# Cross attention scores with the keys on partitions, instead of queries on partitions and transposed probabilities

## The chip, the cores and the metric

The kernel runs on one core of a Trainium2 chip. The time is device microseconds of one execution of the whole program. Timed three times, the kernel before took 3029.02, 3022.6 and 3023.99 us, median 3023.99 us.

## The reference, cut to what matters

A decoder block with three residual parts, each followed by a layer norm: causal self attention (32 heads of 16), cross attention, and a feed forward with a gated low-rank part. The batch is 4 sequences of 256 queries and width 512. The change touches the cross attention alone: 32 heads of 128, 8 key and value heads, 1601 context rows.

```python
scale = 1.0 / sqrt(HDIM)                                   # HDIM = 128
q = (query @ Wq + bq).reshape(B, L, NKV, G, HDIM)          # L = 256, NKV = 8, G = 4
k_, v_ = split(kv @ Wkv + bkv, 2)                          # kv: 1601 rows
scores = einsum('blkgd,bmkd->bkglm', q, k) * scale
attn = softmax(scores)
o = einsum('bkglm,bmkd->blkgd', attn, v)
return o.reshape(B, L, NHEAD * HDIM) @ Wo + bo
```

## The kernel before, in words

One batch element after the other (`for b in range(nb)`), each in three stages: self attention, cross attention, feed forward. Five engines work from programs of their own (`block.tensor` for PE, `block.scalar` for ACT, `block.vector` for DVE, `block.gpsimd` for POOL, `block.sync` for SP, which issues the DMAs) and meet only at semaphores. An engine takes its instructions in order: a wait holds everything behind it.

In the cross attention almost every product is made of three matmuls in fp32r, high times high, high times low, low times high (`mm`, L960). So each operand is split: ACT writes the high part and DVE the low part. The matmuls are grouped in jobs, each into one PSUM bank of a ring of three (`RING`, `freed`): K jobs (keys, four per key head, 12 matmuls of 400 columns), V jobs (values, 13 per pair of key heads, 12 of 256 columns), Q jobs (one per head, 12 of 256), O jobs (output, two per two heads, 6 of 512). `run_job` (L1079) is PE's part, `job_high` (L630) ACT's, `job_low` (L806) DVE's.

A head passes through seven slots `s`, each for two tiles of 128 keys (the last slot has one tile, of 65). The order of jobs and slots is written out by `slot_jobs`.

- `scores` (L1063): queries on partitions, 128 queries at a time, 24 matmuls of 400 or 402 columns per head into four banks (`sp4`).
- `reduce_pair` (L832, the reduce is L837): DVE takes the negative maximum over 800 keys, four times per head; `exponent_bias` (L844) joins them.
- `exponentials` (L652, the activation is L657): ACT writes exp(scale*s - scale*max) to `pbuf`, four passes of 800 columns per head, which also give the row sums.
- `turn_weights` (L1124, L1132): PE transposes the probabilities, 26 tiles of 128x128 per head, so that the keys lie on partitions. ACT makes `ph` (L684), DVE makes `pl` (L884), 512 columns per slot.
- `weigh` (L1136): 39 matmuls of 256 columns per head sum into the one bank `dn`. ACT copies it out (`take_heads_sum`, L666), DVE multiplies by the reciprocals of the sums (`normalize`, L860), which PE spreads over the partitions by two transposes (`spread_reciprocals`, L1159). POOL then adds the bias and splits the result (`finish_head`, L509 to L522).

While the first batch element is worked on, POOL and SP also split the weights of the cross attention into high and low parts, three pieces per head for the first 23 heads (`split_weight`, L499 to L507).

## Time and profile before

| | us |
|---|---|
| median of three runs | 3023.99 |
| the profiled execution | 3015.1 |
| its span, first to last instruction | 3013.3 |
| PE busy | 2897.0 |
| DVE busy | 1778.3 |
| ACT busy | 1448.1 |
| POOL busy | 519.2 |

"PE" counts matmuls, "PEld" the loads of the stationary operand that run beside them. A matmul's duration is a latency: its successor starts long before it ends. The time that a matmul costs is the distance between two starts, which the prediction calls its pitch; for DVE and ACT too a successor can start a little before the predecessor's end. The granted clock is that of TensorE, 1.00 is 2.4 GHz and 0.50 is 1.2 GHz.

### The profile page before, as it was taken

Reading aid. Unit: us, or ns where it says so; the run is one execution under the profiler, and the core shown is the slowest. Engines: PE = TensorE matmul, PEld = TensorE weight load, DVE = VectorE, ACT = ScalarE, POOL = GpSimd, SP = SyncE. Lnnn points to the kernel's source line nnn. Section 1 sums busy time; section 2 is a strip of 40 time slices with the busy share of each in tenths; the row PEclk is TensorE's granted clock in tenths of the full one; section 3 lists DMA queues with packets and bytes.
Section 4 is the critical chain, followed back from the end, with each engine's and each line's share of the span. In section 5 each row is a group of like instructions: output and inputs, shape, how many; then the busy total and the mean of one; then the engine's idle time right before and its main releaser. Section 6 shows DMA issues by size and latency. Waiting matters only on the chain.

```text
span 3013.3 us, 54054 instructions
## 1 busy us (share of the span) xinstructions
PE 2897.0 (96%) x20400; PEld 2727.9 (91%) x20400; DVE 1778.3 (59%) x3596; ACT 1448.1 (48%) x3368; POOL 519.2 (17%) x639
## 2 busy tenths in 40 slices
PE   7899999998899999999889999999988999999997
PEld 6799999998689999999778999999977899999995
DVE  5466666655656565665564656565656565656564
ACT  5454444444545444544364545444536454545453
POOL 4233443301101011111120101010112010101011
PEclk9999999999999999999999999999999999999998
DMA  5455555413212121211321212121232121212113
GB/s 196 141 183 199 182 202 177 164 50 143 89 37 71 57 78 64 78 64 63 127 88 34 71 57 85 57 78 64 78 116 90 36 78 50 79 56 85 57 50 108
DMA packets 97870, 284.69 MB, mean 94 GB/s; under 512 B 9936, under 2 KB 18256, under 8 KB 94416
## 3 DMA queue, kind: packets, MB, share of 16 engines
q1 hardware_dynamic: 97616, 281.24, 27.2%
q8 instruction: 168, 2.75, 0.4%
q14 instruction: 86, 0.70, 0.1%
HBM read 237.16 MB, written 44.04 MB: 93 GB/s over the span
## 4 chain that ended last, share of the span: by engine, by line
PE 91%; DVE 2%; issue 2%; ACT 2%; DMA 1%; POOL 1%; SPq 0%; ACTq 0%; DVEq 0%; POOLq 0%
PE bank L960 36%; PE sp L960 21%; PE dn L960 21%; PE bank L1132 12%; PE bank L1159 1%; PE sp L1031 1%; ACT pn L608 1%; DVE nmx L780 1%; DMA wqk<-in_ws 0%; PE sp L966 0%; ACT pt L614 0%; DVE pn L789 0%; DVE xres L728 0%; DVE stats L719 0%; DMA raw<-in_ctx_t 0%
## 5 line engine op out<-in xcount | busy, mean ns | idle before, releaser
L684 ACT ACTIVATE ph<-bank 128x512 fp32r<-128x512 f32 (+1 forms) x896 | 504.6, 567 | 693.2 <-PE bank L1132 689.7
L884 DVE TENSOR_TENSOR pl<-bank,ph 128x512 fp32r<-128x512 f32 (+1 forms) x896 | 580.2, 648 | 158.0 <-ACT ph L684 146.8
L837 DVE TENSOR_REDUCE mneg<-sp 128x1 f32<-128x800 f32 (+1 forms) x512 | 507.4, 992 | 81.1 <-PE sp L960 61.6
L960 PE MATMUL dn<-ph,vh 128*128 128x256 f32 (+1 forms) x1664 | 541.8, 326 | 0.0
L1132 PE MATMUL bank<-cst,pbuf 128*128 128x128 f32 (+1 forms) x3328 | 509.4, 272 | 1.4
L657 ACT ACTIVATE pbuf<-sp,mb 128x800 f32<-128x800 f32 (+1 forms) x512 | 470.8, 929 | 27.5 <-DVE mb L844 27.4
L960 PE MATMUL dn<-ph,vl 128*128 128x256 f32 (+1 forms) x1664 | 465.4, 280 | 0.0
L960 PE MATMUL dn<-pl,vh 128*128 128x256 f32 (+1 forms) x1664 | 464.8, 279 | 0.0
L1132 PEld LDWEIGHTS bank<-cst,pbuf 128*128 128x128 f32 (+1 forms) x3328 | 404.2, 140 | 41.1 <-DVE pl L884 6.1
L518 POOL TENSOR_SCALAR orw<-orw,cst 128x256 f32<-128x256 f32 x128 | 118.6, 927 | 1768.6 <-DVE orw L860 1768.6
L960 PE MATMUL sp<-kh,qh 128*128 128x400 f32 (+1 forms) x1024 | 363.5, 355 | 5.2 <-issue 4.8
L960 PE MATMUL sp<-kl,qh 128*128 128x400 f32 (+1 forms) x1024 | 354.2, 346 | 0.0
L960 PE MATMUL sp<-kh,ql 128*128 128x400 f32 (+1 forms) x1024 | 352.1, 344 | 0.0
L960 PEld LDWEIGHTS dn<-pl,vh 128*128 128x128 f32 (+1 forms) x1664 | 316.3, 190 | 0.0
L960 PEld LDWEIGHTS dn<-ph,vh 128*128 128x128 f32 (+1 forms) x1664 | 314.6, 189 | 0.3
L960 PEld LDWEIGHTS dn<-ph,vl 128*128 128x128 f32 (+1 forms) x1664 | 312.5, 188 | 0.0
L960 PE MATMUL bank<-wvx,ctxh 128*128 128x256 f32 (+1 forms) x1664 | 298.4, 280 | 0.0
L960 PE MATMUL bank<-ctxh,wk 128*128 128x400 f32 (+1 forms) x1024 | 290.5, 346 | 3.1 <-DVE xres L804 3.1
L960 PEld LDWEIGHTS bank<-wvx,ctxh 128*128 128x128 f32 (+1 forms) x1664 | 254.6, 184 | 0.0
L960 PE MATMUL bank<-wvx,ctxl 128*128 128x256 f32 (+1 forms) x832 | 234.2, 282 | 0.0
L639 ACT ACTIVATE kh<-bank,cst 128x400 fp32r<-128x400 f32 (+1 forms) x128 | 76.4, 597 | 307.1 <-PE bank L960 307.1
L820 DVE SCALAR_TENSOR_TENSOR kl<-bank,cst,kh 128x400 fp32r<-128x400 f32 (+1 forms) x128 | 81.1, 634 | 239.2 <-ACT kh L639 239.2
(126 smaller groups left out, 4841.9 us busy)
## 6 DMA issues: line engine op xcount, KB each, us to landing
wqx<-wq SPq DMA_DIRECT2D x128, 512.0 KB, 3.3
wox<-wo SPq DMA_DIRECT2D x64, 1024.0 KB, 4.9
wk<-wk SPq DMA_DIRECT2D x32, 512.0 KB, 3.3
wvx<-wv SPq DMA_DIRECT2D x16, 1024.0 KB, 5.7
raw<-in_ctx_t SPq DMA_DIRECT2D x48, 200.0 KB, 2.5
wqk<-in_ws SPq DMA_DIRECT2D x17, 513.0 KB, 3.9
raw<-in_wq_in SPq DMA_DIRECT2D x32, 256.0 KB, 3.7
wq<-hib SPq DMA_DIRECT2D x32, 256.0 KB, 2.0
```

What stands on the lines that cost most here:

```text
L518: nc.gpsimd.tensor_scalar(o, o, bias, None, ALU.add).then_inc(oh_ok, 1)
L608: nc.scalar.activation(pn[:, n % 3, a:z], s_bank[n % 5][:, a:z], ACT.Exp, bias=nmx[:, n % 3, qb:qb + 1], accum_out=sm[:, n % 3, qb:qb + 1] ...
L639: nc.scalar.activation(kh[:, a:a + n], src[:, 0:n], ACT.Identity, bias=cst[:, 2 * p + C_BK + kv:2 * p + C_BK + kv + 1]).then_inc(*done)
L657: nc.scalar.activation(pbuf[:, n % 2, tb, key:key + w], spf[:, col:col + w], ACT.Exp, bias=mb[:, n % 2, tb:tb + 1], scale=XSCALE, accum_ou ...
L684: nc.scalar.activation(ph[0:rows, k % PH, 0:cols], ring_bank(b, "turn", h, s)[0:rows, 0:cols], ACT.Copy).then_inc(hi_ok, 1)
L780: nc.vector.tensor_reduce(nmx[:, n % 3, qb:qb + 1], s_bank[n % 5][:, a:z], AX.X, ALU.max, negate=True).then_inc(s_mx, 1)
L820: nc.vector.scalar_tensor_tensor(kl[:, a:a + n], src[:, 0:n], cst[:, 2 * p + C_BK + kv:2 * p + C_BK + kv + 1], kh[:, a:a + n], ALU.add, AL ...
L837: nc.vector.tensor_reduce(mneg[:, n % 2, tb, pair:pair + 1], spf[:, col:col + w], AX.X, ALU.max, negate=True).then_inc(mx_ok, 1)
L884: nc.vector.tensor_tensor(pl[0:rows, k % PH, 0:cols], ring_bank(b, "turn", h, s)[0:rows, 0:cols], ph[0:rows, k % PH, 0:cols], ALU.subtract ...
L960: return nc.tensor.matmul(dst, lhs, rhs, start=first, stop=final)
L1031: last = nc.tensor.transpose(s_turn[:, z:z + P], pn[:, (n - 2) % 3, a:a + P], ident)
L1132: last = nc.tensor.transpose(bank[r % RING][0:w, col:col + P], pbuf[:, n % 2, tb, i * P:i * P + w], ident)
```

## The change

Scores are now computed with the keys on partitions: `kh` and `kl` tiles of 128 keys are stationary, the 256 queries of the head move, 39 matmuls per head. Each slot's scores go into one of two banks. ACT copies them to SBUF (`kept_s`); DVE keeps a running maximum over the key blocks (`mxa`). At the head's end PE transposes `mxa` (four transposes), DVE reduces it (`mcol`), PE spreads the maxima over all partitions (two transposes) and ACT copies them to `mrow`. POOL subtracts `mrow` from the kept scores, slot by slot. ACT then takes the exponential twice: into `ph` (rounded to fp32r) and in full into one of two PSUM banks (`pbank`). DVE makes `pl` from the two and adds the block to a running sum `sua`. Four fp32 matmuls with one moving column of ones give the row sums. `turn_weights` and the 26 transposes of probabilities per head are gone. The ring of banks for jobs goes from three to two, `ph` and `pl` from three to four buffers.

The order of all engines is now a list of slots `g`, 239 per batch element; every step of head h and slot s stands at `g = 7*h + s + offset`: scores at -13, subtraction at -4, exponentials at -3, low part and sum at -2, `weigh` at 0. The steps done once per head have fixed places too (`MAX_TURN` and the others). DVE takes a job's low part one slot after PE runs the job. The weight pieces of the first batch element are placed at slots 0, 2 and 4 of each head, for POOL and for SP, and Q jobs run one head earlier than before.

The diff, cut to its core (lines left out at "..."):

```diff
-RING = 3
-PH = 3
+RING = 2
+PH = 4
...
-    + [("Q", 0, 1)] + [("V", 0, i) for i in range(5, KT)]
+KEYS = [[(i, LAST if i == KT - 1 else P) for i in (2 * s, 2 * s + 1) if i < KT] for s in range(NSL)]
+SCORE, SHIFT, EXP, LOW, VALUE = -13, -4, -3, -2, 0
+MAX_TURN, MAX_COL, MAX_ROW, SUM_COL, SUM_ROW, HEAD_SUM, HEAD_END = -6, -5, -4, 5, 6, 7, 8
+SLOTS = range(SCORE, NSL * (NHB - 1) + HEAD_END + 1)
+def slot_of(g, start):
+    h, s = divmod(g - start, NSL)
+    return [(h, s)] if 0 <= h < NHB else []
+def head_of(g, start):
...
+O_SLOTS = [(3, 3, 5), (2, 5, 6), (2, 5, 6), (3, 1, 3)]
+def jobs_by_slot():
+    jobs = {g: [] for g in SLOTS}
+    for i in range(KT):
+        jobs[SCORE + i].append(("V", 0, i))
+    for p in range(1, NP):
+        for i in range(KT):
+            jobs[NSL * (NHD * p - 1) + 1 + i * 10 // 12].append(("V", p, i))
+    for c in range(1, XKV):
+        for j, (head, s) in enumerate(((-3, 4), (-3, 5), (-3, 6), (-2, 1))):
+            jobs[NSL * (G * c + head) + s].append(("K", c // 2, c % 2 * len(KCH) + j))
+    for h in range(1, NHB):
+        jobs[NSL * h + SCORE - 6].append(("Q",) + divmod(h, NHD))
+    for k in range(NHB // 2 - 1):
+        after, *slots = O_SLOTS[k % 4]
+        for tb, s in enumerate(slots):
+            jobs[NSL * (2 * k + after) + s].append(("O", k // 4, 2 * (k % 4) + tb))
     return jobs
-def ring_uses():
...
-        pbuf = sb("pbuf", [P, 2, TB, LKP])
+        kept_s = sb("kept_s", [P, 2, KT, S])
...
+        bank = [ctx.enter_context(nc.psum_tensor(f"bank{i}", [P, 512], F32)) for i in range(3)]
...
+        sbank, pbank, mbank = [bank[2][:, :], sp4[:, 0, :]], [sp4[:, 1, :], sp4[:, 2, :]], sp4[:, 3, :]
...
+            def shift_scores(b, h, s):
+                n = b * NHB + h
+                i, z = 2 * s, 2 * s + len(KEYS[s])
+                pool.wait_ge(mr_ok, n + 1)
+                pool.wait_ge(cp_ok, n * NSL + s + 1)
+                nc.gpsimd.tensor_tensor(kept_s[:, n % 2, i:z, :], kept_s[:, n % 2, i:z, :],
+                                        mrow[:, n % 2, :].unsqueeze(1).broadcast_to([P, z - i, S]), ALU.subtract).then_inc(sb_ok, 1)
...
+                for g in SLOTS:
+                    for h, s in slot_of(g, SHIFT):
+                        shift_scores(b, h, s)
+                    for h in head_of(g, HEAD_END):
+                        finish_head(b, h)
+                    h, s = divmod(g, NSL)
+                    if b == 0 and 0 <= h < NHB and s in PIECE_SLOTS:
+                        k = NM * SA_W + HEAD_W * h + PIECE_SLOTS.index(s)
+                        if k < W_N:
                             split_weight(k)
...
+                def keep_scores(h, s):
                     n = b * NHB + h
-                    act.wait_ge(mb_ok, at(n, TB, tb + 1))
-                    for pair, (col, key, w) in enumerate(PAIR_AT):
-                        nc.scalar.activation(pbuf[:, n % 2, tb, key:key + w], spf[:, col:col + w], ACT.Exp,
-                                             bias=mb[:, n % 2, tb:tb + 1], scale=XSCALE,
-                                             accum_out=sums[:, n % 2, tb, pair:pair + 1]).then_inc(exp_ok, 1)
+                    k = n * NSL + s
+                    src, dst = sbank[k % 2], kept_s[:, n % 2, 2 * s:2 * s + len(KEYS[s]), :].rearrange("p t q -> p (t q)")
+                    act.wait_ge(sc_mm, k + 1)
+                    if s == NSL - 1:
+                        nc.scalar.activation(dst, src[:, 0:S], ACT.Identity, bias=cst[:, C_TAIL:C_TAIL + 1]).then_inc(cp_ok, 1)
+                    else:
+                        nc.scalar.activation(dst, src[:, :], ACT.Copy).then_inc(cp_ok, 1)
+                def keep_max(h):
+                    n = b * NHB + h
+                    act.wait_ge(mr_mm, n + 1)
+                    if n >= 2:
+                        act.wait_ge(sb_ok, (n - 1) * NSL)
+                    nc.scalar.activation(mrow[:, n % 2, :], mbank[:, 0:S], ACT.Copy).then_inc(mr_ok, 1)
+                def exponentials(h, s):
+                    n = b * NHB + h
+                    k, cols = n * NSL + s, S * len(KEYS[s])
+                    src = kept_s[:, n % 2, 2 * s:2 * s + len(KEYS[s]), :].rearrange("p t q -> p (t q)")
+                    act.wait_ge(sb_ok, k + 1)
+                    if k >= PH:
+                        act.wait_ge(pv_mm, k - PH + 1)
+                    nc.scalar.activation(ph[:, k % PH, 0:cols], src, ACT.Exp, scale=XSCALE).then_inc(ph_ok, 1)
+                    if k >= 2:
+                        act.wait_ge(su_ok, k - 1)
+                    nc.scalar.activation(pbank[k % 2][:, 0:cols], src, ACT.Exp, scale=XSCALE).then_inc(pr_ok, 1)
...
+                for g in SLOTS:
+                    for h in head_of(g, HEAD_SUM):
+                        take_heads_sum(h)
+                    for h, s in slot_of(g, SCORE):
+                        keep_scores(h, s)
+                    for h in head_of(g, MAX_ROW):
+                        keep_max(h)
+                    for h, s in slot_of(g, EXP):
+                        exponentials(h, s)
+                    for j in JOBS[g]:
+                        if j[0] != "O":
+                            job_high(*j)
                 deviation(b, 1)
...
+                def maximum(h, s):
                     n = b * NHB + h
-                    dve.wait_ge(sc_mm, at(n, 4, 2 * tb + pair + 1))
-                    col, _, w = PAIR_AT[pair]
-                    nc.vector.tensor_reduce(mneg[:, n % 2, tb, pair:pair + 1], spf[:, col:col + w], AX.X, ALU.max,
-                                            negate=True).then_inc(mx_ok, 1)
-                def exponent_bias(h, tb):
+                    k, cols = n * NSL + s, S * len(KEYS[s])
+                    dve.wait_ge(cp_ok, k + 1)
+                    if s == 1:
+                        dve.wait_ge(tm_mm, n)
+                        last = kept_s[:, n % 2, 0:2, :].rearrange("p t q -> p (t q)")
+                    else:
+                        dve.wait_ge(mx_ok, n * (NSL - 1) + s - 1)
+                        last = mxa[:, 0:cols]
+                    if s == NSL - 1:
+                        nc.vector.tensor_tensor(mxa[0:LAST, 0:cols], sbank[k % 2][0:LAST, 0:cols], mxa[0:LAST, 0:cols],
+                                                ALU.max).then_inc(mx_ok, 1)
+                    else:
+                        nc.vector.tensor_tensor(mxa[:, 0:cols], sbank[k % 2][:, 0:cols], last, ALU.max).then_inc(mx_ok, 1)
+                def row_maxima(h):
                     n = b * NHB + h
-                    dve.wait_ge(mx_ok, at(n, 4, 2 * tb + 2))
-                    nc.vector.tensor_scalar(mb[:, n % 2, tb:tb + 1], mneg[:, n % 2, tb, 0:1], mneg[:, n % 2, tb, 1:2], XSCALE,
-                                            ALU.min, ALU.mult).then_inc(mb_ok, 1)
+                    dve.wait_ge(tm_mm, n + 1)
+                    dve.wait_ge(mr_mm, n)
+                    nc.vector.tensor_reduce(mcol[:, :], mbank.rearrange("p (a n) -> p a n", a=TB), AX.X, ALU.max).then_inc(mc_ok, 1)
+                def low_and_sum(h, s):
+                    n = b * NHB + h
+                    k, cols = n * NSL + s, S * len(KEYS[s])
+                    src = pbank[k % 2][:, 0:cols]
+                    dve.wait_ge(pr_ok, k + 1)
+                    dve.wait_ge(ph_ok, k + 1)
+                    if k >= PH:
+                        dve.wait_ge(pv_mm, k - PH + 1)
+                    nc.vector.tensor_tensor(pl[:, k % PH, 0:cols], src, ph[:, k % PH, 0:cols], ALU.subtract).then_inc(pl_ok, 1)
+                    if s == 0:
+                        dve.wait_ge(sx_mm, n)
+                        nc.vector.tensor_copy(sua[:, 0:cols], src).then_inc(su_ok, 1)
+                    else:
+                        dve.wait_ge(su_ok, k)
+                        nc.vector.tensor_tensor(sua[:, 0:cols], src, sua[:, 0:cols], ALU.add).then_inc(su_ok, 1)
                 def row_reciprocals(h):
                     n = b * NHB + h
-                    dve.wait_ge(exp_ok, at(n, 4, 4))
-                    nc.vector.tensor_reduce(ssum[:, n % 2, :], sums[:, n % 2, :, :], AX.X, ALU.add).then_inc(rs_ok, 1)
-                    dve.wait_ge(rs_ok, at(n, 2, 1))
-                    nc.vector.reciprocal(rs[:, n % 2, :], ssum[:, n % 2, :]).then_inc(rs_ok, 1)
+                    dve.wait_ge(sx_mm, n + 1)
+                    dve.wait_ge(rd_mm, n)
+                    nc.vector.reciprocal(rs[:, :], mbank[:, 0:TB]).then_inc(rs_ok, 1)
                 def normalize(h):
                     n = b * NHB + h
...
+                for g in SLOTS:
+                    for j in JOBS.get(g - 1, ()):
+                        job_low(*j)
+                    for h, s in slot_of(g, LOW):
+                        low_and_sum(h, s)
+                    for h in head_of(g, MAX_COL):
+                        row_maxima(h)
+                    for h in head_of(g, SUM_COL):
+                        row_reciprocals(h)
+                    for h in head_of(g, HEAD_SUM):
+                        normalize(h)
+                    for h, s in slot_of(g, SCORE):
+                        if s:
+                            maximum(h, s)
                 for j in LAST_JOBS:
                     job_low(*j)
...
+                def scores(h, s):
                     n = b * NHB + h
                     p = h // NHD
-                    pe.wait_ge(exp_ok, at(n, 4, 2 * tb + pair - 1))
-                    pe.wait_ge(freed, ring(b, "job", "Q", p, h % NHD) + RING + 1)
+                    k = n * NSL + s
+                    if k >= 2:
+                        a, z = divmod(k - 2, NSL)
+                        pe.wait_ge(cp_ok, k - 1)
+                        pe.wait_ge(mx_ok, a * (NSL - 1) + z)
+                    pe.wait_ge(freed, ring(b, "Q", p, h % NHD) + RING + 1)
                     if h % G == 0:
-                        pe.wait_ge(freed, ring(b, "job", "K", p, h % NHD // G * len(KCH) + 2 * pair + 1) + RING + 1)
-                    q = slice(tb * P, (tb + 1) * P)
-                    for col, key, w in SP_AT[2 * pair:2 * pair + 2]:
-                        dst = spf[:, col:col + w]
-                        mm(dst, qh[:, h % G, q], kh[:, key:key + w], True, False)
-                        mm(dst, ql[:, h % G, q], kh[:, key:key + w], False, False)
-                        last = mm(dst, qh[:, h % G, q], kl[:, key:key + w], False, True)
+                        pe.wait_ge(freed, ring(b, "K", p, h % NHD // G * len(KCH) + chunk_of(s)) + RING + 1)
+                    for e, (i, w) in enumerate(KEYS[s]):
+                        dst, keys = sbank[k % 2][0:w, e * S:(e + 1) * S], slice(i * P, i * P + w)
+                        mm(dst, kh[:, keys], qh[:, h % G, :], True, False)
+                        mm(dst, kh[:, keys], ql[:, h % G, :], False, False)
+                        last = mm(dst, kl[:, keys], qh[:, h % G, :], False, True)
                     last.then_inc(sc_mm, 1)
+                def turn_maxima(h):
+                    n = b * NHB + h
+                    pe.wait_ge(mx_ok, (n + 1) * (NSL - 1))
+                    if n >= 2:
+                        pe.wait_ge(nm_ok, n - 1)
+                    for tb in range(TB):
+                        for e in range(2):
+                            col = (2 * tb + e) * P
+                            last = nc.tensor.transpose(mbank[:, col:col + P], mxa[:, e * S + tb * P:e * S + (tb + 1) * P], ident)
+                    last.then_inc(tm_mm, 1)
+                def spread_maxima(h):
+                    n = b * NHB + h
+                    pe.wait_ge(mc_ok, n + 1)
+                    for tb in range(TB):
+                        last = nc.tensor.transpose(mbank[:, tb * P:(tb + 1) * P], mcol[:, tb:tb + 1].broadcast_to([P, P]), ident)
+                    last.then_inc(mr_mm, 1)
+                def sum_rows(h):
+                    n = b * NHB + h
+                    pe.wait_ge(su_ok, (n + 1) * NSL)
+                    pe.wait_ge(mr_ok, n + (2 if h + 1 < NHB else 1))
+                    for tb in range(TB):
+                        for e in range(2):
+                            last = mm(mbank[:, tb:tb + 1], sua[:, e * S + tb * P:e * S + (tb + 1) * P], cst[:, C_ONE:C_ONE + 1],
+                                      e == 0, e == 1)
+                    last.then_inc(sx_mm, 1)
...
-                def turn_weights(h, s):
-                    n, r = b * NHB + h, ring(b, "turn", h, s)
...
+                for g in SLOTS:
+                    for h, s in slot_of(g, SCORE):
+                        scores(h, s)
+                    for h in head_of(g, MAX_ROW):
+                        spread_maxima(h)
+                    for h in head_of(g, SUM_ROW):
+                        spread_reciprocals(h)
+                    for j in JOBS[g]:
+                        run_job(*j)
+                    for h, s in slot_of(g, VALUE):
+                        weigh(h, s)
+                    for h in head_of(g, MAX_TURN):
+                        turn_maxima(h)
+                    for h in head_of(g, SUM_COL):
+                        sum_rows(h)
                 for j in LAST_JOBS:
```

## Rows read from the trace of the kernel before

**Rows 1.** Chain that ended last: share of the span by engine.
```profile
PE 91%; DVE 2%; issue 2%; ACT 2%; DMA 1%; POOL 1%; SPq 0%; ACTq 0%; DVEq 0%; POOLq 0%
```
**Rows 2.** Windows: one element's head stage, then eight heads of elements 0 and 1.
```profile
core 0: us, PE busy (x) PEld busy (x) DVE busy (x) ACT busy (x) POOL busy (x), PEclk, DMA share, GB/s
866.60:1476.30 609.70, 609.25 (x4424) 593.24 (x4424) 370.46 (x652) 294.31 (x624) 64.03 (x93) 1.00 0.19 66
...
446.32:601.66 155.34, 155.28 (x1126) 151.33 (x1126) 93.86 (x166) 74.00 (x158) 56.49 (x67) 1.00 0.50 175
1035.57:1190.91 155.34, 155.28 (x1127) 151.34 (x1126) 93.85 (x166) 73.99 (x158) 16.52 (x24) 1.00 0.20 69
```
**Rows 3.** Timeline of PE, 256 and 400 columns: start us, duration us, instruction.
```profile
404.49 0.35 PE L960 MATMUL sp<-kh,qh 128*128 128x400 f32 x1
...
406.69 0.35 PE L960 MATMUL bank<-ctxh,wk 128*128 128x400 f32 x1
...
868.88 0.40 PE L960 MATMUL bank<-wvx,ctxh 128*128 128x256 f32 x2
...
875.97 0.34 PE L960 MATMUL sp<-kh,qh 128*128 128x400 f32 x1
```
**Rows 4.** Timeline of PE: four transposes, `weigh` after them, four fp32 matmuls.
```profile
400.77 0.60 PE L1132 MATMUL bank<-cst,pbuf 128*128 128x128 f32 x4
401.12 0.37 PE L960 MATMUL dn<-ph,vh 128*128 128x256 f32 x1
401.33 0.28 PE L960 MATMUL dn<-pl,vh 128*128 128x256 f32 x1
...
19.83 0.61 PE L960 MATMUL bank<-wv,xt 128*128 128x128 f32 x4
```
**Rows 5.** Timeline of DVE, instructions back to back.
```profile
470.38 0.69 DVE L884 TENSOR_TENSOR pl<-bank,ph 128x512 fp32r<-128x512 f32 x1
470.99 0.41 DVE L860 TENSOR_TENSOR orw<-bank,orw 128x256 f32<-128x256 f32 x1
471.41 0.99 DVE L837 TENSOR_REDUCE mneg<-sp 128x1 f32<-128x801 f32 x1
```
**Rows 6.** Timeline of ACT, instructions back to back.
```profile
445.65 0.60 ACT L684 ACTIVATE ph<-bank 128x512 fp32r<-128x512 f32 x1
446.14 0.93 ACT L657 ACTIVATE pbuf<-sp,mb 128x800 f32<-128x800 f32 x1
446.95 0.20 ACT L657 ACTIVATION_READ_ACCUMULATOR pbuf<-sp,mb 128x1 f32 x1
```
**Rows 7.** Groups by shape, POOL: busy us, mean ns, idle before.
```profile
L507 POOL TENSOR_TENSOR lob<-raw,hib 128x512 fp32r<-128x512 f32 x80 | 103.5, 1294 | 6.4
...
L522 POOL TENSOR_TENSOR ol<-orw,oh 128x256 fp32r<-128x256 f32 x128 | 94.7, 740 | 11.0
```
**Rows 8.** Timeline, last head of element 1: last `weigh` matmul, its copy, the multiplication.
```profile
1475.96 0.28 PE L960 MATMUL dn<-ph,vl 65*128 65x256 f32 x1
...
1476.28 0.38 ACT L666 ACTIVATE orw<-dn 128x256 f32<-128x256 f32 x1 [1.38 <-PE dn L960]
...
1476.69 0.42 DVE L860 TENSOR_TENSOR orw<-bank,orw 128x256 f32<-128x256 f32 x1 [1.34 <-ACT orw L666]
```
**Rows 9.** Timeline: PE resumes after waiting for DVE's `ql`.
```profile
121.46 0.48 DVE L825 SCALAR_TENSOR_TENSOR ql<-bank,cst,qh 128x256 fp32r<-128x256 f32 x1 [0.73 <-ACT qh L645]
122.04 0.42 PE L960 MATMUL sp<-kh,qh 128*128 128x400 f32 x1 [1.20 <-issue]
122.30 0.34 PE L960 MATMUL sp<-kh,ql 128*128 128x400 f32 x1
```
**Rows 10.** Windows: self attention, and after the wait at a stage's end.
```profile
20.00:100.00 80.00, 64.91 (x492) 53.36 (x491) 56.45 (x184) 52.90 (x193) 38.52 (x40) 1.00 0.58 180
...
1476.30:1480.00 3.70, 0.60 (x4) 0.43 (x3) 0.42 (x1) 1.64 (x2) 2.04 (x3) 1.00 1.04 428
1480.00:1484.00 4.00, 4.00 (x12) 2.91 (x10) 0.69 (x1) 0.00 (x0) 0.00 (x0) 0.57 0.87 358
```

More of the change, by code:

```diff
@@ L120 @@
+JOBS = jobs_by_slot()
+JOB_AT = {j: i for i, j in enumerate(FIRST_JOBS + [j for g in SLOTS for j in JOBS[g]] + LAST_JOBS)}
 NJ = len(JOB_AT)
@@ L161, in raw_of_weight @@
     return NM * len(SA_RAW) + k - NM * SA_W
-def head_pieces(h):
-    first = NM * SA_W + HEAD_W * h
-    return range(min(first, W_N), min(first + HEAD_W, W_N))
 NSH = NM * HB
@@ L1272, in lay_out @@
     consts[:, C_EPS] = EPS
+    consts[LAST:, C_TAIL] = NEG
+    consts[:, C_ONE] = 1.0
     consts[:, C_BK:C_BK + XKV] = i["L0_xattn_bkv"][:XKV * XD].reshape(XKV, XD).T
```

291 lines of the change are left out of this document (91 added, 200 removed).

## The prediction, made before the changed kernel was run

> **What bounds the kernel now.** I read the chain of waits first: 91% of the span is PE [rows 1]. Then the windows. The cross attention's head stage of one batch element, from the first scores to the last spread of reciprocals, lasts 609.7 us, and PE is busy for 609.25 of them at full clock; eight heads take 155.34 us, 19.4 each, the same in element 0 and element 1 [rows 2]. DVE is busy for 60% of that, ACT for 48%, POOL for 11% (36% in element 0). So what the stage costs is the sum of PE's pitches, and every other engine is hidden. Four such stages are 2439 of 3013 us, and the change is inside them alone.
>
> Pitches of PE: 12 score matmuls of 400 columns lie between 404.49 and 406.69, 0.183 us each; 60 of 256 columns between 868.88 and 875.97, 0.118 each [rows 3]. Four transposes take 0.35 us to the next start, and the matmul behind them costs 0.21 instead of 0.12, so a group is 0.44 and a pair 0.22 [rows 4].
>
> **What PE saves.** Per head, out: six groups of four transposes and one pair, 6 x 0.44 + 0.22 = 2.86 us. Scores: 24 x 0.183 = 4.39 become 39 x 0.118 = 4.60, plus 0.21. In: four transposes of `mxa` 0.44, two of `mcol` 0.22, and `sum_rows`. For its fp32 matmuls with one column no row exists. Four fp32 matmuls of 128 columns take 0.61 us, a latency of 0.28 included, so 0.11 each, 0.53 with the changeover [rows 4]; the lower end is the transposes' 0.35 for four. I take 0.50. Net: -2.86 + 0.21 + 0.44 + 0.22 + 0.50 = -1.49 us per head, 48 us per element, 191 us in all. PE's work in a stage falls from 610 to 562 us. This is the whole possible gain.
>
> **What the others get.** DVE is busy 93.9 / 8 = 11.7 us per head [rows 2]. Out go four reduces of 0.99 and small ones of 0.57 together. In come six maxima and seven sums. Two 512-column passes in a row cost 0.61 each, not the 0.69 of their duration [rows 5], and the passes of 256 columns 0.34: 3.4 + 4.0 us. The reduce of 512 columns is 0.99 less 288 columns at (0.69 - 0.41) / 256, about 0.7. That gives 15.3 us per head, 80% of what a head takes. ACT: 74 / 8 = 9.3, less four exponentials of 0.9 and seven high parts of 3.3 together, plus seven copies (3.3), `mrow` (0.3) and fourteen exponentials. One of 512 columns lies between 0.52 (0.81 for 800, scaled) and 0.60 (a whole copy) [rows 6]; I take 0.57: 13.6 us. POOL: 16.5 / 8 = 2.1 for `finish_head` [rows 2], plus 6 x 1.29 + 0.74 = 8.5 for the subtraction [rows 7]: 10.6. In element 0 the weight pieces add (56.5 - 16.5) / 8 = 5.0: 15.6.
>
> No engine passes PE on the average of 562 / 32 = 17.6 us. But PE's work is uneven: a head with no jobs but Q has about 12 us of it, the head with eight V jobs 23, and the other engines keep nearly the same load in all. In a light slot PE has 1.4 us (two times six matmuls), DVE 1.8 (three passes). Two score banks bind them: PE may start slot g only when DVE has finished slot g-2.
>
> **The new waits of PE.** I stepped the schedule through, slot by slot: each instruction starts when its engine is free and its semaphores are in, with the pitches above and 0.06 us per semaphore. It adds these, per element:
> - Reciprocals. `spread_reciprocals` stands in the slot after `sum_rows`, behind six score matmuls (0.70). From the sum on, DVE first does the copy that starts the next head's `sua`, because that copy waits for `sum_rows` too, and then the reciprocal: 0.23 for the matmul's latency beyond its pitch and a semaphore, 0.61, the reciprocal 0.15, and the way back to PE 0.15: 1.15 us. PE waits 0.45, 32 times: 14 us.
> - The bank `dn`. `weigh` of the next head starts one slot after the last `weigh`; between stand only three score matmuls. The copy starts 0.32 us after the last matmul does and lasts 0.38 [rows 8], and ACT can be inside an exponential. The wait is 0.3 to 2 us, 0.65 on the mean, 28 times: 18 us. Before, two slots of other work stood in between.
> - DVE late with a maximum or a low part: in three of eight heads, and above all in the 13 slots behind the last scores, where PE has 12 us of work and DVE two passes per slot. Together 12 us.
> - Each wait costs a restart: PE's first pitch after one is 0.26 instead of 0.18, and it starts 0.10 after DVE's end [rows 9]. 85 x 0.09 = 8 us.
>
> Sum: 562 + 52 = 614 against 610, so +4 us per element, +16 in all. In element 0, POOL's 15.6 us stand beside heads of 15.3 to 16.6 us, and its lateness reaches ACT: +4. DMAs: SP waits for the same jobs as before, but a Q load is issued a head earlier, and the pieces stand two slots apart instead of one behind the other; the self attention and feed forward stages are not touched. I cost these at nothing, hidden by two heads of distance. What ends up on the profiled execution's 3015.1 us is +20, 3035 us; the median of the runs stands 9 us higher, so 3042 is the number I give for a median.
>
> **Two rules weighed.** DVE's rows show a successor starting 0.61 us after a pass that lasts 0.69 [rows 5]. The Trainium skill, VectorE: DVE Perf Modes, section "The DRAIN you can't avoid", says that the next operation starts only when the pipe has emptied. By that rule every pass would cost its duration, rival B below; the rows before speak against it. The other is the clock. In self attention PE is busy 81% of the time, the rest in many waits, and the granted clock stays at 1.00; after 3.1 us of idleness at a stage's end it is 0.57, partly at the 1.2 GHz level [rows 10]. The Trainium skill, TensorE: Matmul & The Clock Gate, section "A second HAM failure mode: psum-queue depth-cycling", says that frequent short idles between groups of matmuls make the clock swing. By it this change would lose clock, rival C; the row at 81% speaks against it, since I expect 91%.
>
> **Rivals.**
> - Forecast: gain on PE's pitches, given back in waits; -5 to +55 us. 48%.
> - A, faster: the waits are hidden better than I step them, with semaphores of 0.03 us and no restart cost: 604 us per element, -20 in all. If DVE cost nothing at all, the stepping gives -72; the saved work of 191 us is never reached, because ACT's and POOL's links remain. Time: 2990 to 3018. For it: 191 us of PE work really go, and idle time on DVE and ACT remains. 28%.
> - B, slower through DVE: with several semaphores per pass and its own chains (`sua`, `mxa`), a pass costs 0.69. Then DVE has 16.5 us per head and the light heads go by DVE; the stepping gives 630 us per element, +82, so 3124. It decides from a pitch of 0.63 on: each 0.02 us adds 15. For it: three semaphores stand before each low part, where the rows have passes behind one. Against it: the rows. 20%.
> - C, the clock: a few per cent of the matmuls at half speed, +50 to +150. 4%.
> - The change would not do what it says only in that fp32 matmuls with one column cost far more than 0.11, say 0.25 each: +0.5 us per head, +60. It is within the range, for B's numbers.
>
> **How the numbers follow.** Faster by over 0.2% (6 us, about what a measurement of this kernel can tell) takes A and a piece of the forecast's lower end: 0.30. Within: 0.15. Slower: 0.55. The range leaves out A's far end and half of B and C: 2990 to 3115 us.
>
> **What would show it.** PE busy in a head stage falls to about 91% of it, its work to 562 us. Waits of PE `dn` for ACT's `orw` copy, about 0.65 us, once per head, and of the spread for DVE's `rs`, 0.45 us. DVE's passes 0.61 us apart when back to back; DVE busy near 15 us per head and POOL's subtraction at 1.29 us. Heads with V jobs near 24 us, heads without jobs near 15 to 16. I am wrong if PE's waits per stage are under 40 us or over 70, if `sum_rows` takes over 0.8 us, or if the granted clock inside the stage leaves 1.00.

## The result and the profile after

The changed kernel took 3050.99 us (median of 4 runs, 3042.88 to 3052.90), the kernel before beside it 3023.30 us (4 runs, 3015.25 to 3029.02). The ratio is 1.0087, with a 95% interval of 1.0070 to 1.0104: slower, by less than 1%. The prediction said 3042, slower, and 3051 lies within its range. The profiled execution took 3042.88 us, its span 3041.1, so the spans differ by 27.8 us where the steps gave 20.

The page of the kernel after, parts 1 and 4 (busy time, and the chain that ended last); the chain answers to [rows 1].

```profile
PE 2831.5 (93%) x20784; PEld 2619.2 (86%) x20784; DVE 2171.2 (71%) x4492; ACT 1906.0 (63%) x4264; POOL 1570.0 (52%) x1535
...
PE 78%; issue 7%; ACT 6%; POOL 3%; DVE 3%; DMA 2%; DVEq 0%; SPq 0%; ACTq 0%; POOLq 0%
```

PE's part in the chain falls from 91% to 78%, and what took its place is issue, ACT, POOL and DVE: not one new bound, but many small links. The windows of the kernel after say where the time is: the head stages of elements 0 to 3, first scores to last spread of reciprocals (in the kernel after, three `weigh` matmuls stand behind that spread, and the window ends with them). They answer to the first of [rows 2]. (Columns: window, its length, then the busy time and the number of instructions of PE, PEld, DVE, ACT and POOL, the granted clock, the DMA share, GB/s.)

```profile
124.10:744.90 620.80, 592.59 (x4520) 566.80 (x4520) 469.26 (x876) 409.24 (x847) 453.14 (x453) 1.00 0.47 158
881.10:1495.70 614.60, 591.98 (x4520) 565.31 (x4520) 468.76 (x876) 408.52 (x847) 327.38 (x317) 1.00 0.21 71
1631.90:2246.60 614.70, 592.10 (x4520) 565.30 (x4520) 468.74 (x876) 408.57 (x847) 327.49 (x317) 1.00 0.20 71
2382.90:2997.60 614.70, 592.11 (x4520) 565.38 (x4520) 468.87 (x876) 408.55 (x847) 327.42 (x317) 1.00 0.19 67
```

Four stages of 609.7 became 620.8 and three of about 614.7: 11.1 + 4.9 + 5.0 + 5.0 = 26 of the 27.8 us. Per head DVE is busy 468.8 / 32 = 14.6 us, ACT 12.8, POOL 10.2 (14.2 in element 0), where the prediction has 15.3, 13.6, 10.6 and 15.6. The granted clock rounds to 1.00 in all four; the places inside them where it is lower come below, under rival C. PE counts as busy for 592 us, which is more than the sum of its pitches: a matmul's recorded duration runs on for 0.16 us behind its pitch, so every wait is partly covered by "busy" in this column. The waits themselves, in element 1's stage (who waited for whom, us in total, times, longest):

```profile
PEld dn L1012 <- ACT orw L713: 20.2, 28, 1.0
PEld sp L1232 <- DVE rs L917: 8.8, 32, 0.9
PEld sp L1143 <- DVE mxa L883: 4.9, 10, 0.8
PEld sp L1151 <- DVE mcol L893: 2.2, 2, 1.8
```

I read them at PEld, the weight load, because it is the first thing that a waiting group of matmuls issues: 36 us in four places, those that were forecast, and 5.5 us in scraps, 41.6 in all. Before, the same rows of a head stage add up to 3.4 us. The timeline of PE shows the first two and the new fp32 matmuls (start us, duration us, then what it idled for).

```profile
1053.31 0.95 PE L1012 MATMUL sp<-cst,sua 128*128 128x1 f32 x8
1054.12 0.36 PE L1012 MATMUL bank<-qh,kh 128*128 128x256 f32 x1
1054.32 0.28 PE L1012 MATMUL bank<-ql,kh 128*128 128x256 f32 x1
...
1054.78 0.28 PE L1012 MATMUL bank<-qh,kl 128*128 128x256 f32 x1
1055.12 0.43 PE L1232 MATMUL sp<-cst,rs 128*128 128x128 f32 x2
...
1486.57 0.28 PE L1012 MATMUL dn<-ph,vl 65*128 65x256 f32 x1
1487.33 0.38 PE L1012 MATMUL dn<-ph,vh 128*128 128x256 f32 x1 [0.47 <-ACT orw L713]
```

`sum_rows` writes four matmuls, and the trace has eight records of them, from 1053.31 to 1054.12: 0.81 us, and the next matmul's pitch is 0.20 instead of 0.115. That is 0.90 us per head where the prediction has 0.50. The spread of the reciprocals starts at 1055.12 where 1054.90 was its turn. Across the boundary of two heads, 1486.57 to 1487.33, PE loses 0.64 us to the copy out of bank `dn`.

### The profile page after: what moved, and what is told of

It reads as the page before. It is cut to its first block, busy times and chain, and to the rows that moved or that the text cites. A ratio compares the mean times of both kernels' runs of the same rounds, so it can differ in the third digit from the quotient of the medians.

```text
span 3041.1 us, 60253 instructions
## 1 busy us (share of the span) xinstructions
PE 2831.5 (93%) x20784; PEld 2619.2 (86%) x20784; DVE 2171.2 (71%) x4492; ACT 1906.0 (63%) x4264; POOL 1570.0 (52%) x1535
## 4 chain that ended last, share of the span: by engine, by line
PE 78%; issue 7%; ACT 6%; POOL 3%; DVE 3%; DMA 2%; DVEq 0%; SPq 0%; ACTq 0%; POOLq 0%
PE bank L1012 41%; PE dn L1012 18%; PE sp L1012 14%; PE sp L1143 2%; ACT ph L702 2%; POOL kept_s L524 1%; ACT orw L713 1%; PE sp L1232 1%; PE sp L1083 1%; PE sp L1151 1%; ACT pn L629 1%; POOL lob L516 1%; DVE nmx L819 1%; POOL orw L536 0%; DMA wqk<-in_ws 0%
## 5 line engine op out<-in xcount | busy, mean ns | idle before, releaser
L524 POOL TENSOR_TENSOR kept_s<-kept_s,mrow 128x512 f32<-128x512 f32 (+1 forms) x896 | 1061.1, 1214 | 539.8 <-ACT mrow L692 539.8
L904 DVE TENSOR_TENSOR pl<-sp,ph 128x512 fp32r<-128x512 f32 (+1 forms) x896 | 577.0, 644 | 43.3 <-ACT sp L705 42.8
L702 ACT ACTIVATE ph<-kept_s 128x512 fp32r<-128x512 f32 (+1 forms) x896 | 534.8, 597 | 35.1 <-POOL kept_s L524 30.3
L705 ACT ACTIVATE sp<-kept_s 128x512 f32<-128x512 f32 (+1 forms) x896 | 506.3, 565 | 3.5 <-DVE sua L910 2.2
L910 DVE TENSOR_TENSOR sua<-sp,sua 128x512 f32<-128x512 f32 (+1 forms) x768 | 487.7, 635 | 0.0
L684 ACT ACTIVATE kept_s<-bank 128x512 f32<-128x512 f32 x384 | 229.0, 596 | 330.6 <-PE bank L1012 330.6
L684 ACT ACTIVATE kept_s<-sp 128x512 f32<-128x512 f32 x384 | 229.6, 598 | 254.8 <-PE sp L1012 254.8
L1012 PE MATMUL bank<-qh,kh 128*128 128x256 f32 (+1 forms) x832 | 245.2, 295 | 10.1 <-DVE ql L864 5.2
L1012 PE MATMUL sp<-qh,kh 128*128 128x256 f32 (+1 forms) x832 | 243.2, 292 | 0.2
L1012 PE MATMUL sp<-qh,kl 128*128 128x256 f32 (+1 forms) x832 | 232.9, 280 | 0.0
```

What stands on the lines that cost most here:

```text
L524: nc.gpsimd.tensor_tensor(kept_s[:, n % 2, i:z, :], kept_s[:, n % 2, i:z, :], mrow[:, n % 2, :].unsqueeze(1).broadcast_to([P, z - i, S]), ...
L684: nc.scalar.activation(dst, src[:, :], ACT.Copy).then_inc(cp_ok, 1)
L702: nc.scalar.activation(ph[:, k % PH, 0:cols], src, ACT.Exp, scale=XSCALE).then_inc(ph_ok, 1)
L705: nc.scalar.activation(pbank[k % 2][:, 0:cols], src, ACT.Exp, scale=XSCALE).then_inc(pr_ok, 1)
L904: nc.vector.tensor_tensor(pl[:, k % PH, 0:cols], src, ph[:, k % PH, 0:cols], ALU.subtract).then_inc(pl_ok, 1)
L910: nc.vector.tensor_tensor(sua[:, 0:cols], src, sua[:, 0:cols], ALU.add).then_inc(su_ok, 1)
```

## The experiments

Two theories stand against each other, and every expectation names both. Theory 1 is the prediction's: PE's pitches plus the short loops through other engines that PE must wait for, `dn` (ACT), `rs`, `mxa` and `mcol` (DVE), with `sum_rows` at 0.90. Theory 2 has the stage set by the rate at which DVE, ACT and POOL get through their work, the waits being only where that shows. All edits are to the kernel after, except in the last. The ratios are to the kernel before, timed beside each version. In the tables of windows a "stage" is that of element 1, as above.

### The Q job between two heads

```
-        jobs[NSL * h + SCORE - 6].append(("Q",) + divmod(h, NHD))
+        jobs[max(SCORE, NSL * h + SCORE - 8)].append(("Q",) + divmod(h, NHD))
```

SCORE - 6 is -19, slot 2 of a head; -21 is slot 0, where the job stands ahead of the head's first `weigh`.

> The changed kernel with one edit: each Q job (12 matmuls, 1.4 us of PE) stands in the slot in which PE now waits for the copy out of the bank dn, two slots earlier than in the change. Theory 1, PE's waits are serial links that other PE work could cover: the wait of the next head's weigh for the copy, 20 us per batch element in the trace of the changed kernel, and its restarts all but vanish, and nothing else replaces them: 15 to 25 us per element, 60 to 90 us in all, 2960 to 2990 us. Theory 2, DVE's passes set the rate and PE's wait is only where it shows: within 10 us of the changed kernel's 3050, with PE's waits moved to the running maximum. In between, since the slot behind is lighter: -30 to -50.

2998.67 us (2993.67 to 3008.06), ratio 0.9924 (0.9898 to 0.9950). The stage:

```profile
868.20:1470.00 601.80, 587.02 (x4516) 564.97 (x4516) 464.67 (x877) 406.94 (x847) 327.71 (x317) 1.00 0.21 72
```

Its waits over the whole span, and under them those of the kernel after:

```profile
PEld sp L1151 <- DVE mcol L893: 43.4, 60, 1.8
...
PEld dn L1012 <- ACT orw L713: 10.2, 17, 1.0
```

```profile
PEld dn L1012 <- ACT orw L713: 86.6, 112, 2.0
PEld sp L1232 <- DVE rs L917: 36.1, 128, 1.0
PEld sp L1143 <- DVE mxa L883: 18.6, 38, 0.8
PEld sp L1151 <- DVE mcol L893: 9.0, 8, 1.8
```

PE does the same work in another order, and 12.8 us per element go, 52 us in all. That is less than the 60 to 90 of theory 1, which expected that nothing would replace the wait for `dn`, and just past the 30 to 50 given for a case in between. The wait for `dn` falls by 76 us, but the wait for `mcol` grows by 34. That is the other side of the same move: slot 2 lies between the turn of the maxima (end of slot 1) and their spread (slot 3), so the job had been the cover of DVE's reduce, and that was its price. A theory of rates alone has no place for either number; the engines' busy times hardly move.

### The reduce of the maxima ahead of the low part on DVE

```
+                    for h in head_of(g, MAX_COL):
+                        row_maxima(h)
                     for h, s in slot_of(g, LOW):
                         low_and_sum(h, s)
-                    for h in head_of(g, MAX_COL):
-                        row_maxima(h)
```

with the Q job moved as above.

> The moved Q jobs again, and on DVE the reduce of the transposed maxima now stands ahead of the low part and sum of its slot instead of behind them. With the Q jobs moved, PE waited 43 us in all for that reduce (31 us of them visible on PE), a wait that came when the slot ahead of the spread lost its Q job. Theory 1, serial links: it goes, 25 to 40 us off the 2999 of the moved Q jobs alone, 2960 to 2975. Theory 2, DVE's rate: the same DVE work in another order gives back less than 10 us, 2990 or more.

2984.37 us (2976.35 to 2985.78), ratio 0.9864 (0.9840 to 0.9887).

```profile
873.40:1469.80 596.40, 587.19 (x4520) 565.75 (x4520) 463.65 (x876) 406.42 (x847) 327.60 (x317) 1.00 0.21 73
```

The wait for `mcol` falls from 43.4 to 2.5 us in the span, and the stage is 5.4 us shorter. The time is above what theory 1 expected and below what theory 2 did. Part of what is missing shows as waits that had come to 1.1 us in the span with the Q job moved alone, for ACT's copy of the scores out of the bank:

```profile
PEld sp L1012 <- ACT kept_s L684: 11.4, 28, 0.5
PEld bank L1012 <- ACT kept_s L684: 10.8, 49, 0.3
```

PE's score matmuls need a bank that ACT has copied. While PE was held elsewhere, the copy was nearly always in time.

### The reciprocal ahead of the copy that starts the next sum

```
                     for h in head_of(g, SUM_COL):
                         row_reciprocals(h)
+                    for h, s in slot_of(g, LOW):
+                        if s == 0:
+                            first_sum(h, s)
```

where `first_sum` is the `tensor_copy` to `sua` that `low_and_sum` did in slot 0; alone first, with the Q job where the change has it.

> The changed kernel with one edit: DVE takes the reciprocal of the row sums before, not after, the copy that starts the next head's running sum. No instruction is added or removed. Theory 1: PE's wait for the reciprocals (9 us per element with 32 restarts of 0.09, so 12) goes, 47 us in all at most, 20 to 45 expected since part of it comes back as a wait for DVE's maximum. Theory 2, DVE's rate: no change, within 8 us, since DVE has the same work.

3032.96 us (10 runs, 3028.12 to 3037.41), ratio 1.0025 (1.0014 to 1.0037), 18 us under the change: short of the 20 to 45 of theory 1, and more than twice the 8 of theory 2.

```profile
884.90:1495.50 610.60, 587.66 (x4520) 564.65 (x4520) 468.67 (x876) 408.62 (x847) 327.45 (x317) 1.00 0.21 72
```

The wait for `rs` falls from 36.1 to 2.8 us; in its place `mxa` rises from 18.6 to 23.6 and waits for `kept_s` appear, the largest with 9.0:

```profile
PEld sp L1149 <- DVE mxa L883: 23.6, 40, 0.8
...
PEld bank L1018 <- ACT kept_s L684: 9.0, 32, 0.3
```

This element gains 4.0 us of the 8.8 that PE waited in it.

### The three moves together

> All three moves: Q jobs two slots earlier, DVE's reduce of the maxima ahead of the low part, DVE's reciprocal ahead of the copy. Theory 1: the gains add, about 12.9 us per element for the first, 6 to 10 for the second, 3.5 to 5 for the third: 588 to 593 us per element and 2945 to 2965 in all, which would be 2% under the kernel before. Theory 2: they overlap, 2975 or more, with waits for the running maximum in their place.

2962.94 us (2958.68 to 2965.07), ratio 0.9794 (0.9775 to 0.9813); the stage:

```profile
865.00:1457.90 592.90, 583.27 (x4516) 565.36 (x4517) 463.79 (x877) 406.16 (x847) 327.71 (x317) 1.00 0.21 73
```

That is inside what theory 1 expected, for the stage and for the time. 21.7 us of the stage are gone, by order alone: the instructions are those of the change. Of 41.6 us of waits in the stage 20.2 are left, above all for `kept_s` (24 + 17 us in the span), `orw` (12) and `mxa` (11).

### Half the row sums

The loop `for e in range(2)` of `sum_rows` runs once, so each row sum covers about half of the keys.

> The changed kernel with the row sums taken over one half of the keys only: two of the four fp32 matmuls with one column per head are left out, so the output's scale is off. In the trace they cost 0.81 us per head for what I had taken as 0.41. If PE's pitches plus its waits make the stage (theory 1), leaving two out takes 0.4 us from each head: 128 x 0.4 = 51 us, 2995 to 3010 us. If DVE sets the rate (theory 2), less than 15 us.

2998.85 us (2997.13 to 3002.32), ratio 0.9916 (0.9894 to 0.9938).

```profile
877.60:1477.80 600.20, 577.13 (x4390) 550.47 (x4391) 468.90 (x877) 408.61 (x847) 328.00 (x317) 1.00 0.21 72
```

52 us under the change, as theory 1 expected. Two matmuls less per head, four records: 14.4 / 32 = 0.45 us, against 0.40 from the timeline, and PE's waits stay what they were (41.8 us in the stage, 41.6 before the edit). So the fp32 matmuls of one column lie wholly on the path, at 0.20 to 0.22 us each.

### POOL's subtraction halved

`i, z = 2 * s, 2 * s + 1` in POOL's subtraction: the first key tile of each pair alone; the second keeps its unshifted scores.

> The changed kernel with POOL's subtraction on the first key tile of each slot only: the second tile keeps its unshifted scores, so the output is not the reference's; POOL has 4.2 us less per head. Theory 1 with POOL as the cause of element 0's longer stage (620.8 us against 614.6 of the others): element 0 falls to about 615, the others stay within 1 us: 5 to 8 us in all. Rival: the splitting of weights, its stores or SP's order delay element 0 in another way: element 0 stays at 620. Second rival: the link POOL to ACT is on the path in every element: all four fall, by 5 us or more each.

3042.77 us (3041.10 to 3045.13), ratio 1.0057 (1.0036 to 1.0078). Elements 0 and 1:

```profile
131.50:746.00 614.50, 591.93 (x4520) 565.24 (x4520) 468.84 (x876) 406.94 (x847) 349.68 (x453) 1.00 0.47 160
882.00:1496.10 614.10, 591.50 (x4519) 564.85 (x4520) 468.80 (x876) 406.94 (x847) 221.91 (x317) 1.00 0.20 71
```

8 us under the change, the upper end of what theory 1 gave. POOL does some 104 us less in each element. Element 0 loses its 6.2 us of excess, element 1 only 0.5. So POOL's rate costs in element 0, where the weight pieces stand beside the subtraction, and hardly anywhere else; not all of the 6.2 us is POOL's, as the part on element 0 below shows. The waits of the kernel after in element 0's stage show the same:

```profile
POOL kept_s L524 <- ACT mrow L692: 89.1, 22, 26.2
...
ACT ph L702 <- POOL kept_s L524: 24.3, 21, 4.6
```

In element 1 POOL waits 150 us for `mrow`, and ACT 2.0 us for POOL: POOL has time there that it lacks in element 0.

### The running sum's adds cut to 8 columns

```
-                        nc.vector.tensor_tensor(sua[:, 0:cols], src, sua[:, 0:cols], ALU.add).then_inc(su_ok, 1)
+                        nc.vector.tensor_tensor(sua[:, 0:8], src[:, 0:8], sua[:, 0:8], ALU.add).then_inc(su_ok, 1)
```

The row sums then miss most of their terms.

> The changed kernel with the running sum's adds cut from 512 columns to 8 (six of seven per head), so the row sums are wrong; DVE has about 3 us less per head, PE and ACT the same instructions. Theory 1: DVE is late in few places only, so the stage of an element falls from 614.5 by 5 to 12 us, 20 to 50 in all, and the wait for the copy out of dn stays at about 20 us per element. Theory 2, DVE's rate sets the stage: it falls by 30 us or more per element.

3013.08 us (6 runs, 3009.03 to 3017.62), ratio 0.9967 (0.9953 to 0.9980).

```profile
874.30:1479.20 604.90, 587.18 (x4518) 564.18 (x4518) 385.37 (x877) 408.69 (x847) 327.05 (x317) 1.00 0.20 71
```

38 us under the change. 83 us of DVE's work per element bring 9.7 us of time, as theory 1 expected (5 to 12). If DVE's rate had set the stage, most of the 83 would have come out, and the stage would have met PE's own work, some 573 us. The waits that stay are the serial ones: `dn` at 84.7 us and `rs` at 35.8 in the span, as in the change. What goes is DVE being late: `mxa` and `mcol` fall from 27.6 us in the span to 4.7.

### One pass of DVE for two fp32 matmuls

The three moves, and:

```
+                    if s == NSL - 1:
+                        dve.wait_ge(su_ok, k + 1)
+                        nc.vector.tensor_tensor(sua[:, 0:S], sua[:, S:2 * S], sua[:, 0:S], ALU.add).then_inc(fd_ok, 1)
...
-                        for e in range(2):
+                        for e in range(1):
```

`sum_rows` waits for `fd_ok` instead of `su_ok`.

> The three moves, and before the row sums DVE adds the two halves of its running sum once per head (one pass of 256 columns between two SBUF tiles), so that PE needs two fp32 matmuls with one column instead of four. PE saves 0.41 to 0.45 us per head, DVE gets about 0.35 more. Theory 1 (PE's pitches): 12 to 14 us per element less than the three moves alone, 50 us in all. If DVE's rate now binds: less than 15 us in all, or slower. Rival in the chip: a DVE pass with two SBUF inputs and POOL's subtraction hold each other up; then the pass or the subtraction beside it lasts visibly longer than 0.4 and 1.29 us.

2928.58 us (2926.11 to 2931.81), ratio 0.9689 (0.9671 to 0.9707): 3.1% under the kernel before and 4% under the change.

```profile
856.40:1440.30 583.90, 571.69 (x4391) 552.43 (x4392) 489.64 (x908) 406.14 (x847) 333.51 (x317) 1.00 0.21 75
```

9.0 us per element instead of the 12 to 14 expected. The stage's waits at PEld rose from 20.2 to 23.7 us, 2.8 of them for this pass (10.4 in the span, new); without the waits the stage is 12.5 us shorter, as expected. The groups by shape show what the pass cost (busy us, mean ns, idle before), and two rows of DVE's timeline how far it varies:

```profile
L524 POOL TENSOR_TENSOR kept_s<-kept_s,mrow 128x512 f32<-128x512 f32 x768 | 988.3, 1320 | 449.5 <-ACT mrow L692 448.9
...
L910 DVE TENSOR_TENSOR sua<-sua 128x256 f32<-128x256 f32 x128 | 108.7, 849 | 4.4
...
L907 DVE TENSOR_TENSOR sua<-sp,sua 128x256 f32<-128x256 f32 x128 | 52.6, 411 | 0.0
...
549.23 0.43 DVE L910 TENSOR_TENSOR sua<-sua 128x256 f32<-128x256 f32 x1
2840.97 1.55 DVE L910 TENSOR_TENSOR sua<-sua 128x256 f32<-128x256 f32 x1
```

The same 256 columns cost 411 ns with one input in PSUM and 849 on the mean with both in SBUF, and POOL's subtraction goes from 1293 to 1320. The pass at 549.23 us ran while POOL was idle (from 547.67 to 549.97 us) and took 0.43, and so did, within 0.01 us, the four others that met an idle POOL; the one at 2840.97 ran beside POOL's subtractions and took 1.55. So the extra time is the rival named in the expectation: the two passes hold each other up.

### The removed transposes, priced in the kernel before

```
-                        for tb in range(TB):
+                        for tb in range(1 if b else TB):
```

in the kernel before's `turn_weights`: elements 1 to 3 turn one of the two row tiles only, and the other's weights are stale.

> The kernel before, with the weights of only one of the two row tiles turned in elements 1 to 3 (element 0 turns both), so that half of the attended values there are made from stale weights. It prices the term of the sum that was removed, 0.44 us per group of four transposes and 0.22 per pair. Theory 1 (the head stage of the kernel before costs the sum of PE's pitches, every other engine hidden): two of four transposes go from six groups, one of two from the last, so 6 x 0.22 + 0.11 = 1.43 us per head, 46 us per element; three elements, 137 us: the time goes to about 2886, element 0 stays at 609.7 and elements 1 to 3 fall to about 564. Theory 2 (the transposes were partly cover for the two exponential parts on ACT and DVE, so that taking them away turns into waits there too): the elements fall by under 35 us, the time stays above 2915.

2892.81 us (2890.68 to 2893.42) against 3020.57, ratio 0.9576 (0.9559 to 0.9593). Element 1's stage:

```profile
875.00:1441.10 566.10, 564.39 (x4005) 547.61 (x4006) 360.53 (x653) 291.89 (x623) 63.91 (x93) 1.00 0.21 71
```

The time is near the 2886 of theory 1 and far from the 2915 of theory 2. The stage is 43.6 us shorter than 609.7, 1.36 us per head where the pitches gave 1.43. The rest is a wait that the stage did not have before:

```profile
PEld dn L960 <- DVE pl L884: 2.9, 8, 0.7
```

All waits at PEld in this stage add up to 5.2 us, against 3.4 in the kernel before. Without them the two stages are 560.9 and 606.3 us: 45.4 us, or 1.42 per head. So the kernel before costs the sum of PE's pitches, what is taken from PE comes out but for a small wait, and the prediction's 2.86 us per head for all transposes stands, if the second half of them costs what the first does.

## Why the prediction was right, and where its steps were off

**Direction and mechanism.** Right, and tested: PE's work fell by about one us per head, and more than that came back as waits at the places named. That moving one job by two slots takes 12.8 us off an element, and three changes of order 21.7, is what loops do and rates don't. One count shows it for all versions at once: element 1's stage, less all waits at PEld in it, in us.

| | stage | waits | rest |
|---|---|---|---|
| before | 609.7 | 3.4 | 606.3 |
| after | 614.6 | 41.6 | 573.0 |
| Q job moved | 601.8 | 27.9 | 573.9 |
| and reduce moved | 596.4 | 23.3 | 573.1 |
| reciprocal first | 610.6 | 38.5 | 572.1 |
| three moves | 592.9 | 20.2 | 572.7 |
| adds cut | 604.9 | 33.4 | 571.5 |
| POOL's half | 614.1 | 41.6 | 572.5 |
| half the row sums | 600.2 | 41.8 | 558.4 |
| fold | 583.9 | 23.7 | 560.2 |
| half the transposes | 566.1 | 5.2 | 560.9 |

The rest stays within 571.5 and 573.9 us wherever PE's instructions are the same, and falls by 12.5 and 14.6 us where two fp32 matmuls per head go. So the stage is PE's own work plus its waits. The change took 33.3 us from the work and added 38.2 us of waits.

The forecast of 614 us for elements 1 to 3 met 614.6 to 614.7. That closeness is luck: two errors lie in the sum, 11 us too little for PE's work (562 for 573) and 10 us too much for the waits (52 for 41.6), and they cancel.

**The term that was mis-sized: `sum_rows`.** "Four fp32 matmuls of 128 columns take 0.61 us ... so 0.11 each" read x4 in [rows 4] as four matmuls of the program. It counts records, and `sum_rows` shows that one fp32 matmul leaves two (four in the code, eight in the trace, x1024 in the span for 128 heads). So four of them have eight pitches of 0.10. Measured: 0.81, plus 0.09 for the changeover, 0.90 us per head instead of 0.50; 0.40 x 32 = 13 us per element. Halving them gave back 0.45 of these per head. The prediction set this as a sign of being wrong ("if `sum_rows` takes over 0.8 us"), and it came true. With it the prediction's own terms give 562 + 13 = 575 us for PE's work, 2 more than the table's 573.

**The waits.** Stepped: 52 us with restarts; measured: 36 in the four places and 5.5 in scraps, right at the mark of 40 that the prediction had set.
- `dn`: 18 us and 28 restarts of 0.09, 20.5; measured 20.2, 28 times. Right.
- Reciprocals: 0.45 and a restart, 17 us; measured 8.8, 0.28 each. On the timeline the loop takes 1.00 us from 1054.12 to 1055.12, not 1.15, and the six score matmuls behind `sum_rows` cover 0.78 of it, not 0.70, since the first has the changeover's 0.20.
- DVE late: 12 us and restarts; measured 4.9 for `mxa` and 2.2 for `mcol`.

**Element 0.** +11.1, of which 6.2 more than the others; the prediction had 4. Two causes share it. Counted from the stage's start, the spread of the reciprocals of a head comes later in element 0 than in element 1: by 4.7 us at head 21, reached in steps of about 0.8 while the weights are split, and no more than that up to head 29. This part is POOL's, as the halved subtraction shows. Between heads 29 and 30 another 1.5 us are lost. There the clock was low (see C), so POOL's rate is not the whole cause.

**The sum.** +27.8 on the span instead of +20: 3 us from elements 1 to 3 (5 each, not 4), 3 from element 0, 1.8 outside the stages. The step to a median has a slip: 3035 and 9 are 3044, not 3042. In B, +82 on the kernel before gives 3106; 3124 counts the forecast's own rise a second time. The other three executions of the changed kernel took 7 to 10 us more than the profiled one, at a mean granted clock of 0.983 to 0.984 against 0.985. Estimated from these figures, 0.001 to 0.002 of 3045 us, the clock is 3 to 6 of these us.

**The rivals.** A, waits hidden, was wrong for this change, yet its ground was sound: three changes of order removed half of them. B, DVE at 0.69 per pass, is refuted. The timeline of DVE in the kernel after:

```profile
1054.29 0.69 DVE L907 COPY sua<-sp 128x512 f32<-128x512 f32 x1 [2.75 <-PE sp L1012]
1054.90 0.16 DVE L917 RECIPROCAL rs<-sp 128x2 f32<-128x2 f32 x1
1054.98 0.67 DVE L886 TENSOR_TENSOR mxa<-sp,mxa 128x512 f32<-128x512 f32 x1
1055.57 0.41 DVE L868 TENSOR_TENSOR vl<-bank,vh 128x256 fp32r<-128x256 f32 x1
```

0.61 and 0.59 us from start to start, and cutting 83 us of DVE's work moved a stage by 9.7. By the rule that the prediction quotes from the Trainium skill, VectorE: DVE Perf Modes, section "The DRAIN you can't avoid", the steps would be 0.69 and 0.67; the trace disagrees. The same section goes on, "A next op that is not held starts earlier", which the prediction leaves out; the steps of 0.61 and 0.59 us fit that.

C, the clock, is not refuted: it came true in small. The prediction's sign for it was a granted clock inside the stage that leaves 1.00. It did in element 0, and at the end of every stage (windows of element 0, element 1, and the end of element 1's stage):

```profile
726.00:731.00 5.00, 4.25 (x19) 4.08 (x20) 3.25 (x7) 2.59 (x6) 3.42 (x4) 0.66 0.01 2
1472.00:1484.00 12.00, 8.81 (x64) 7.76 (x63) 9.79 (x19) 8.71 (x19) 9.29 (x11) 1.00 0.01 1
1494.50:1495.70 1.20, 1.07 (x5) 1.03 (x5) 0.07 (x1) 0.00 (x0) 0.00 (x0) 0.54 0.99 393
```

From about 726.7 to 730 us PE runs at the 1.2 GHz level, its 256-column matmuls 0.21 us apart. Just before, it had waited for `orw`, `mxa` and `mcol`, 3.0 us in three pieces. It waited for the same three in element 1, 3.0 us too, before 1479 us, and there the clock stayed at 1.00. So the waits alone do not decide it, and what does was not found. The stage of element 0 with POOL's subtraction halved has no such stretch, so the 6.3 us that it is shorter contain these 1.5; with one profiled execution of each, whether POOL had a part in the fall of the clock is not shown. With half the row sums, element 0 has four such stretches, at 176, 214, 368 and 521 us. At the end of element 1's stage the clock falls at about 1494.5 us, after PE waited for `sua` and `rs`. For the change this is worth 1.5 of its 28 us. It is worth more between single executions: of the ten of `rec_first`, the four at a mean clock of 0.983 took 3035.5 to 3037.4 us, the three at 0.986 and 0.987 took 3028.1 to 3029.5.

The fp32 rival (0.25 per matmul, +60 us) named the right operation; it came to 0.20 each, and the other waits being shorter than stepped made up for it.

What is not settled: why the clock falls in one element and not in the next after the same waits, and the 2 us between 575 and 573. In the version with the fold, 23.7 us of waits are left per element, 12.0 of them for `kept_s`; which slots they stand in was not traced.

## What to carry to other kernels

Where one engine is busy all the time and work is taken from it by giving it to three others, price each loop that leaves the engine and comes back, against what stands between the two ends in that engine's own order. Here the change lost by 28 us, and the same instructions in another order won by 60. To check the price, subtract the waits from the stage: if the rest stays the same when only the order changes, the waits are the whole difference. Look at what a filler job covers before moving it: it may cover two loops, and moving it from one to the other shows the second. Each wait removed brought less than its row said, because the next engine in line was just behind it: 8.1 us of waits for `rs` gone from element 1's stage gave 4.0.

## What the runs showed of the hardware

- An fp32 matmul leaves two records and costs 0.20 us with 128 weight columns even when it moves a single column, as against 0.118 for one of 256 columns in fp32r [rows 3]. Summing over partitions by such a matmul is not cheap for its size: 0.90 us per head for four.
- A DVE pass over 128x256 with both inputs in SBUF took 424 to 1548 ns in the version with the fold, 849 on the mean, where one with an input in PSUM took 411, and POOL's subtractions became longer (1320 ns for 1293). With POOL idle it took 0.42 to 0.43 us, so two inputs in SBUF cost next to nothing by themselves; the rest is what POOL and DVE do to each other. The Trainium skill, SBUF — State Buffer, section "Who interferes with whom", says that a two-input operation with both inputs in SBUF contends with GpSimd's reads; these rows agree with that.
- A wait of PE for another engine costs its first matmul too: 0.22 us to the next start instead of 0.12 at 1487.33 (next start 1487.55), as [rows 9] had it with 0.26 instead of 0.18.
- The granted clock fell to its 1.2 GHz level in the middle of PE's work, at 726.7 us of the kernel after, and did not fall an element later after the same three waits. It cost 1.5 us there: eleven pitches of 256 columns took 0.21 us instead of 0.12. Executions of one kernel differ by it, 3028 to 3037 us with mean clocks of 0.987 to 0.983 (`rec_first`).
